# A decoder block: loading the first image by tiles, its low parts between the normalisations on VectorE, and unread products ahead

## The chip, the cores and the metric

The kernel runs on one core of a Trainium2 chip. The metric is the time of one execution on the device in microseconds, as the median of several runs; lower is better. Engine names: PE is TensorE, DVE is VectorE, ACT is ScalarE, POOL is GpSimd, SP is the engine that issues the transfers.

## What is computed

A decoder block on `x` of 4 images x 512 rows x 512 columns, in f32:

```python
x = x + attn(layernorm(x), Wq, bq, Wk, bk, Wv, bv, Wo, bo)   # 16 heads; attention over the 128 channels of a head
x = x + xattn(layernorm(x), ctx, ctx, gamma)                 # 8 heads
x = x + ffn(layernorm(x), w1, w3, w2)                        # ternary weights, silu(h1) * h3
```

In `attn` the queries are transposed, so that the scores of a head are q^T k over the 512 rows, a 128 x 128 matrix. With n = layernorm(x), these scores are Wq^T (n^T n) Wk and terms of the biases: the kernel first forms the Gram matrix n^T n (512 x 512) of each image and then multiplies it by the weights.

## The kernel before

Products keep f32 accuracy with rounded operands (type fp32r): each operand is split in a high part (ScalarE's copy, rounded) and a low part (operand minus high part), and `three_passes` makes high x high, high x low and low x high, so that lines 163, 164 and 165 stand for all such products. An attention pass takes two images (`PB` = 2); there are two passes, and cross attention and the feed-forward part follow.

The opening, which the change touches, is this, with an image as 4 row tiles j of 128 x 512 and a Gram matrix as 4 column blocks c:

- SP: `sp_rows_in` loads image 0 in two halves of two tiles each, then image 1 the same, then `raw_a` (wk), two rows for the bias, `raw_b` (wq), and more.
- GpSimd makes the identity `ident` (used for transposes later).
- VectorE, `dve_rows`: per tile statistics (`bn_stats`), their aggregate, the inverse root by 13 small dependent steps (`dve_rstd`, one for all four tiles), and then for each tile the normalisation and an addition of `KAPPA` to its first column (`dve_normalise`; this column carries the bias). ScalarE makes each tile's high part `ph` as soon as it is normalised (`act_rows`).
- The low parts `pl` of image 0 are made by VectorE after all four normalisations; those of image 1 by GpSimd (`pool_rows`), tile by tile as ScalarE's high parts come.
- TensorE: `pe_gram` for image 0, then image 1, with c outside and j inside: 4 x 4 x 3 = 48 products of 128 x 512 for an image. In the first block (c = 0) each tile j is waited for.
- The blocks leave PSUM as `gh` (ScalarE, `act_gram`) and `gl` (VectorE, `dve_gram`). ScalarE's order is: `ph` of image 0, `gh` of its blocks 0 and 1, `ph` of image 1, `gh` of blocks 2 and 3, the high part `wah` of wk, `gh` of image 1. VectorE's order: image 0's rows and low parts, image 1's rows, `gl` of image 0, the bias row added to wk (`dve_bias`), the low parts of two of the four blocks of wk (`dve_split_a`; GpSimd makes the other two), `gl` of image 1.
- Then TensorE goes to the products of wk with the Gram matrices (`pe_scores`). Four PSUM banks go round between all these tiles; a bank is free when VectorE has made the low part from it (`a_free`).

In the second pass the rows of both images are normalised between other work, and GpSimd makes all low parts; the change leaves that as it is.

Of the kernel before, what the change touches and what calls it, by code (L numbers as in the profile page):

```python
# [18 lines left out]
F32 = mybir.dt.float32  # L19
# [3 lines left out]
ALU = mybir.AluOpType  # L23
AX = mybir.AxisListType.X

P = 128
B, T, C = 4, 512, 512
CK = C // P
TJ = T // P
NH, HG = 16, 4  # L30
GROUPS = NH // HG
PB = 2
# [103 lines left out]
RSTD_STEPS = 1 + 12  # L136
# [31 lines left out]
def decoder_block(nc, x, ctx, wk, wq, wo, wvt, bk, bq, bv_col, bo, gamma, w1t, w3t, w2t, out):  # L168
# [7 lines left out]
    with stack:  # L176
# [2 lines left out]

        s = {}  # L180
        for name in (
            "ident", "xn_a0", "xn_b0", "xn_a1", "xn_b1", "raw_a", "raw_b", "row_in", "bv_in", "bo_in", "x_in", "wadd_a", "wadd_b",
            "link", "xn", "ph", "pl_dve", "pl_pool", "a_ready", "a_hi", "a_free",
            "wah", "wal_dve", "wal_pool", "wbh", "wbl",
            "s_done", "s_read", "mx", "nmx", "rinv", "dv", "vadd", "att_ready", "att_free", "pth", "ptl",
# [5 lines left out]
            "s_ready", "s_free", "t_ready", "t_free", "r_ready", "r_free",  # L191
            "xmx", "xrinv", "xpn", "pxh", "x3n", "x3h", "link_b",
            "tanh", "gate_sp", "gate_dve", "gate_pool", "y", "y_out",
        ):
            s[name] = sem("s_" + name)
# [121 lines left out]
        def late_bank(n):  # L317
            return bank[6 + n % 2]
# [656 lines left out]
        def sp_rows_in(sp, p, i):  # L975
            one, two = halves(x[PB * p + i])
            sp.dma_start(xnf[i][:, 0:2], one).then_inc(s[f"xn_a{i}"], 16)
            sp.dma_start(xnf[i][:, 2:4], two).then_inc(s[f"xn_b{i}"], 16)

        def sp_slot_a(sp, p, step):  # L980
            wait_raw_a_free(sp, p, step)
            src = wk[step] if step < GROUPS else wo[step - GROUPS]
            sp.dma_start(raw_a[:], src.rearrange("(c p) n -> p c n", p=P)).then_inc(s["raw_a"], 16)
# [161 lines left out]
        @block.sync  # L1145
        def _(sp):
            credit(sp, "sp")
            gate(sp, "sp")
            for i in range(PB):
                sp_rows_in(sp, 0, i)  # L1150
            sp_slot_a(sp, 0, 0)
            sp_row(sp, wk, bk, 0)
            sp_slot_b(sp, 0, 0)
            sp.dma_start(bvc[:], bv_col).then_inc(s["bv_in"], 16)
            for w in range(3):
                sp_magnitudes(sp, 0, w)
            sp.wait_ge(s["wadd_a"], wadd_a(0, 1))
            sp_row(sp, wq, bq, 0)
            sp.dma_start(gam[:], gamma.to_broadcast([P, 1])).then_inc(s["gam_in"], 16)
            sp_scores(sp, 0)  # L1160
            sp_values(sp, 0)
            sp_scores_early(sp)
            sp_values(sp, PASSES - 1)
            stage_b_sp(sp)
# [11 lines left out]
        def pe_gram(pe, p, i):  # L1176
            for c in range(CK):
                u = A["G", p, i, c]
                pe_bank(pe, u)
                for j in range(TJ):  # L1180
                    if c == 0:
                        if p == 0 and i == 0:
                            pe.wait_ge(s["pl_dve"], j + 1)
                        else:
                            pe.wait_ge(s["pl_pool"], TJ * (PB * p + i - 1) + j + 1)
                    mm = three_passes(pe, a_bank(u)[:], ph[:, i, j, c * P:(c + 1) * P], pl[:, i, j, c * P:(c + 1) * P],
                                      ph[:, i, j, :], pl[:, i, j, :], j == 0, j == TJ - 1)
                mm.then_inc(s["a_ready"], 1)
# [191 lines left out]
        def pe_values(pe, p):  # L1380
            for j in range(GROUPS):
# [9 lines left out]
                for i in range(PB):  # L1391
                    if last and further:
                        pe_gram(pe, p + 1, i)
                    for a in range(HG):
                        pe_out(pe, p, j, i, a)
                        if last and not further and i:
                            pe_x3(pe, 0, a)

        @block.tensor
        def _(pe):  # L1400
            pe.wait_ge(s["ident"], 2)
            for i in range(PB):
                pe_gram(pe, 0, i)
            pe_scores(pe, 0)
            pe_values(pe, 0)
            pe_scores_early(pe)
            pe_values(pe, PASSES - 1)
            stage_b_pe(pe)
# [243 lines left out]

        def dve_moments_in(dve, link, p, i, half):

            dve.wait_ge(s[("xn_a", "xn_b")[half] + str(i)], 16 * (p + 1))
            for j in (2 * half, 2 * half + 1):
                ins = dve.bn_stats(bst[:, i, j, :], xnf[i][:, j, :])
            link(ins)

        def dve_aggregate(dve, link, i):  # L1660
            for j in range(TJ):
                ins = dve.bn_aggr(mvar[:, i, j, :], bst[:, i, j, :])
            link(ins)

        def dve_rstd(dve, link, i, k):

            if k == 0:
                link(dve.tensor_copy(nvar[:, i], mvar[:, i, :, 1]))
            else:
                newton_step(dve, link, rstd[:, i], ntmp[:, i], nvar[:, i], k - 1)  # L1670

        def dve_normalise(dve, link, i, j):
            link(dve.tensor_scalar(xnf[i][:, j, :], xnf[i][:, j, :], mvar[:, i, j, 0:1], rstd[:, i, j:j + 1],
                                   ALU.subtract, ALU.mult))
            dve.tensor_scalar(xnf[i][:, j, 0:1], xnf[i][:, j, 0:1], KAPPA, None, ALU.add).then_inc(s["xn"], 1)

        def dve_rows(dve, link, p, i):
            for half in range(2):
                dve_moments_in(dve, link, p, i, half)
            dve_aggregate(dve, link, i)  # L1680
            for k in range(RSTD_STEPS):
                dve_rstd(dve, link, i, k)
            for j in range(TJ):
                dve_normalise(dve, link, i, j)

        def dve_low(dve, dst, high, u):
            dve.wait_ge(s["a_hi"], split(u))
            dve.tensor_tensor(dst, a_bank(u)[:], high.bitcast(F32), ALU.subtract).then_inc(s["a_free"], 1)  # L1688

        def dve_gram(dve, p, i):  # L1690
            for c in range(CK):
                dve_low(dve, gl[i][:, c, :], gh[i][:, c, :], A["G", p, i, c])

        def dve_row(dve, link, p, g, slot):
# [274 lines left out]
        @block.vector  # L1969
        def _(dve):  # L1970
            credit(dve, "dve")
            link = make_link(dve, "link", chain)
            dve_rows(dve, link, 0, 0)
            for j in range(TJ):
                dve.wait_ge(s["ph"], j + 1)
                dve.tensor_tensor(pl[:, 0, j, :], xnf[0][:, j, :], ph[:, 0, j, :].bitcast(F32), ALU.subtract).then_inc(s["pl_dve"], 1)
            dve_rows(dve, link, 0, 1)
            dve_gram(dve, 0, 0)
            dve_bias(dve, link, 0, 0, "a")
            dve_split_a(dve, 0, 0)  # L1980
            dve_gram(dve, 0, 1)
            dve_bias(dve, link, 0, 0, "b")
            dve_scores(dve, link, 0)
            dve_values(dve, link, 0)
            dve_scores_early(dve, link)
            dve_values(dve, link, PASSES - 1)
            stage_b_dve(dve, link)


        def pool_rows(pool, p, i):  # L1990
            for j in range(TJ):
                pool.wait_ge(s["ph"], TJ * (PB * p + i) + j + 1)
                pool.tensor_tensor(pl[:, i, j, :], xnf[i][:, j, :], ph[:, i, j, :].bitcast(F32), ALU.subtract).then_inc(s["pl_pool"], 1)
# [84 lines left out]
        @block.gpsimd  # L2078
        def _(pool):
            credit(pool, "pool")  # L2080
            pool.memset(ident[:], 0.0).then_inc(s["ident"], 1)
            pool.wait_ge(s["ident"], 1)
            pool.affine_select(out=ident[:], in_=ident[:], compare_op=ALU.not_equal, fill=1.0, base=0,
                               pattern=[[-1, P]], channel_multiplier=1).then_inc(s["ident"], 1)
            pool.memset(wsum[:], 0.0).then_inc(s["w_pad"], 1)
            pool_rows(pool, 0, 1)
            pool_split_a(pool, 0, 0)
            pool_split_b(pool, 0, 0)
            pool_scores(pool, 0)
            pool_values(pool, 0)  # L2090
            pool_scores_early(pool)
            pool_values(pool, PASSES - 1)
            stage_b_pool(pool)
# [34 lines left out]
```

## Time and profile before

| | us |
|---|---|
| median of 3 runs | 1137.38 (1136.97 to 1137.83) |
| the profiled execution, its time | 1134.82 |
| the same, its span | 1133.0 |
| TensorE busy in the span | 1108.6 |
| first product of TensorE | 14.01 |
| first product with wk | 37.26 |

The granted clock is 1.00 over the whole span. The span starts a little after the execution, hence the 1.8 us between its time and its span. Starts in the timeline are counted from the start of the span. The products overlap in the pipeline, so a product's pace is the distance of two starts, not its duration.

### The profile page before, as it was taken

The page shows a single profiled execution, that of the slowest core. Times are in us where ns is not written, and L with a number is a line of the kernel's source. Part 1 is how long each engine was busy: PE and PEld are TensorE (multiplying, and loading weights), DVE is VectorE, ACT ScalarE, POOL GpSimd, SP SyncE. Part 2 cuts the span into 40 slices and gives each one's busy share as a digit, 9 for nine tenths or more (in the row PEclk, how much of TensorE's full clock was granted, in tenths as well). Part 3 has the DMA queues.
Part 4 walks back from the last instruction along what each step waited for, and adds up shares of the span by engine and source line. Part 5 has one row for each costly group of instructions (what it writes and reads, how often), then busy time and mean ns, then how long its engine had stood idle before and what let it go on. Part 6 is the DMA issues. An engine that isn't in the chain of part 4 may idle for free.

```text
span 1133.0 us, 15861 instructions
## 1 busy us (share of the span) xinstructions
PE 1108.6 (98%) x5824; PEld 938.8 (83%) x5824; DVE 738.5 (65%) x1376; ACT 544.8 (48%) x1129; POOL 469.1 (41%) x412
## 2 busy tenths in 40 slices
PE   5999999999999999999999999999999999999998
PEld 4888888878888878888888888888888888888886
DVE  7555547787757578775524344689968876888532
ACT  3456673324242365676425142267727762776130
POOL 2222326341332265674352140156626752675131
PEclk9999999999999999999999999999999999999999
DMA  7455543544433722412630202462024111410000
GB/s 241 161 187 184 180 163 136 172 124 170 128 118 106 229 92 92 134 39 84 248 112 1 75 20 96 143 211 67 1 81 122 59 47 41 128 47 1 38 1 38
DMA packets 54376, 122.20 MB, mean 108 GB/s; under 512 B 10025, under 2 KB 10025, under 8 KB 52250
## 3 DMA queue, kind: packets, MB, share of 16 engines
q1 hardware_dynamic: 54298, 121.18, 32.7%
q8 instruction: 47, 0.77, 0.3%
q14 instruction: 31, 0.25, 0.1%
HBM read 103.32 MB, written 17.84 MB: 107 GB/s over the span
## 4 chain that ended last, share of the span: by engine, by line
PE 92%; DVE 4%; ACT 2%; issue 1%; DMA 0%; POOL 0%; DVEq 0%; POOLq 0%; SPq 0%
PE bank L163 19%; PE bank L165 19%; PE bank L164 19%; PE bank L575 6%; PE bank L576 6%; PE bank L535 4%; PE bank L590 4%; PE bank L591 4%; PE bank L557 3%; PE bank L558 2%; PE bank L545 2%; PE bank L546 2%; PE bank L600 1%; PE bank L523 0%; DVE xmx L760 0%
## 5 line engine op out<-in xcount | busy, mean ns | idle before, releaser
L575 PE MATMUL bank<-x3h,w 128*128 128x512 f32 (+2 forms) x368 | 143.3, 393 | 0.6 <-DVE x3l L847 0.3
L576 PE MATMUL bank<-x3l,w 128*128 128x512 f32 (+2 forms) x368 | 140.4, 384 | 0.0
L1420 ACT ACTIVATE yh<-bank 128x512 fp32r<-128x512 f32 x64 | 38.1, 600 | 209.9 <-PE bank L165 209.8
L929 POOL TENSOR_SCALAR pe_x<-pe_x,xri,gam 128x512 f32<-128x512 f32 x96 | 76.5, 797 | 99.1 <-DVE xri L764 95.9
L760 DVE TENSOR_REDUCE xmx<-bank 128x1 f32<-128x512 f32 x128 | 87.6, 686 | 30.8 <-PE bank L546 29.1
L1998 POOL TENSOR_TENSOR wal<-raw_a,wah 128x512 fp32r<-128x512 f32 x44 | 60.4, 1402 | 110.8 <-ACT wah L1442 110.8
L163 PE MATMUL bank<-wah,gh 128*128 128x512 f32 x256 | 102.8, 402 | 2.0 <-DVE wal L1728 2.0
L2003 POOL TENSOR_TENSOR wbl<-raw_b,wbh 128x512 fp32r<-128x512 f32 x64 | 87.6, 1396 | 39.0 <-ACT wbh L1462 38.7
L163 PE MATMUL bank<-yh,rh 128*128 128x512 f32 x256 | 100.2, 392 | 0.8 <-DVE xacc L1857 0.8
L163 PE MATMUL bank<-wah,ph 128*128 128x512 f32 x256 | 100.2, 391 | 0.0
L164 PE MATMUL bank<-wal,gh 128*128 128x512 f32 x256 | 100.1, 391 | 0.0
L165 PE MATMUL bank<-wah,gl 128*128 128x512 f32 x256 | 99.9, 390 | 0.0
L164 PE MATMUL bank<-wal,ph 128*128 128x512 f32 x256 | 99.8, 390 | 0.0
L165 PE MATMUL bank<-yh,rl 128*128 128x512 f32 x256 | 99.7, 389 | 0.0
L164 PE MATMUL bank<-yl,rh 128*128 128x512 f32 x256 | 99.7, 389 | 0.0
L165 PE MATMUL bank<-wah,pl 128*128 128x512 f32 x256 | 99.6, 389 | 0.0
L1688 DVE TENSOR_TENSOR yl<-bank,yh 128x512 fp32r<-128x512 f32 x64 | 44.1, 691 | 84.5 <-ACT yh L1420 84.5
L1857 DVE SCALAR_TENSOR_TENSOR xacc<-bank,rinv,xacc 128x512 f32<-128x512 f32 x64 | 47.9, 749 | 69.3 <-PE bank L165 66.9
L679 ACT ACTIVATE pe_x<-bank,xmx 128x512 f32<-128x512 f32 x96 | 66.1, 688 | 34.8 <-DVE xmx L760 34.5
L575 PEld LDWEIGHTS bank<-x3h,w 128*128 128x128 f32 (+1 forms) x368 | 68.2, 185 | 15.1 <-DVE x3l L847 0.7
L576 PEld LDWEIGHTS bank<-x3l,w 128*128 128x128 f32 (+1 forms) x368 | 68.2, 185 | 12.8
L1688 DVE TENSOR_TENSOR ml<-bank,mh 128x512 fp32r<-128x512 f32 x64 | 43.6, 686 | 53.8 <-ACT mh L1420 53.8
(172 smaller groups left out, 2997.8 us busy)
## 6 DMA issues: line engine op xcount, KB each, us to landing
raw_a<-in_wk SPq DMA_DIRECT2D x8, 1024.0 KB, 5.2
raw_b<-in_wq SPq DMA_DIRECT2D x8, 1024.0 KB, 5.6
raw_a<-in_wo SPq DMA_DIRECT2D x8, 1024.0 KB, 5.1
raw_b<-in_wvt SPq DMA_DIRECT2D x8, 1024.0 KB, 4.9
ternary_scratch<-wraw SPq DMA_DIRECT2D x24, 341.2 KB, 3.1
x1d<-x_scratch SPq DMA_DIRECT2D x48, 128.0 KB, 3.0
kd<-in_ctx SPq DMA_DIRECT2D x48, 128.0 KB, 3.2
w<-ternary_scratch SPq DMA_DIRECT2D x2, 2730.0 KB, 10.8
```

The source lines that it names most:

```text
L163: pe.matmul(out, wh, xh, start=start, stop=False, skip_group_check=shared)
L164: pe.matmul(out, wh, xl, start=False, stop=False, skip_group_check=shared)
L165: return pe.matmul(out, wl, xh, start=False, stop=stop, skip_group_check=shared)
L575: pe.matmul(u_bank[w][0:m, cols], lhs, x3h[:, c, cols], start=c == 0, stop=False)
L576: mm = pe.matmul(u_bank[w][0:m, cols], lhs, x3l[:, c, cols], start=False, stop=c == CK - 1)
L679: act.activation(m.pe_x[:, q, :], m.s[q % 2][:], ACT.Exp, bias=xmx[:, q:q + 1], accum_out=xrs[:, q:q + 1]).then_inc(s["s_free"], 1)
L760: dve.reduce_max(xmx[:, q:q + 1], m.s[q % 2][:], axis=AX, negate=True).then_inc(s["xmx"], 1)
L929: pool.tensor_scalar(m.pe_x[:, q, :], m.pe_x[:, q, :], xri[:, q:q + 1], gam[:], ALU.mult, ALU.mult).then_inc(s["xpn"], 1)
L1688: dve.tensor_tensor(dst, a_bank(u)[:], high.bitcast(F32), ALU.subtract).then_inc(s["a_free"], 1)
L1857: dve.scalar_tensor_tensor(xacc[:, i, a, :], late_bank(n)[:], rinv[:, j, a // 2, q:q + 1], xacc[:, i, a, :], ALU.mult, ALU.add).then_inc(s ...
L1998: pool.tensor_tensor(wal[:, c, :], raw_a[:, c, :], wah[:, c, :].bitcast(F32), ALU.subtract).then_inc(s["wal_pool"], 1)
L2003: pool.tensor_tensor(wbl[:, c, :], raw_b[:, c, :], wbh[:, c, :].bitcast(F32), ALU.subtract).then_inc(s["wbl"], 1)
```

## The change

- Image 0 comes in four transfers, one for each tile, each with its own semaphore; VectorE makes a tile's statistics as it lands. The order on SP is four tiles of image 0, two halves of image 1, and the rest as before.
- `dve_normalise_split`: normalise tile 0, tile 1, then low part 0, normalise 2, low part 1, normalise 3, low part 2, low part 3. It is used for image 0 and for image 1. GpSimd's `pool_rows(0, 1)` is gone; all eight low parts of the first pass are VectorE's.
- VectorE takes `gl` of blocks 0 and 1 of image 0 between the inverse root and the normalisations of image 1; blocks 2 and 3 come after them.
- TensorE, once `ident` is there, makes 22 products of `ident` with itself (unrounded f32, 128 x 128) into a bank that is first used later and whose content nobody reads, and then begins `pe_gram`.

```diff
+        def sp_first_rows(sp):
+
+            tiles = x[0].rearrange("(p j) c -> p j c", j=TJ)
+            for j in range(TJ):
+                sp.dma_start(xnf[0][:, j], tiles[:, j]).then_inc(s[f"xn_t{j}"], 16)
...
-            for i in range(PB):
-                sp_rows_in(sp, 0, i)
+            sp_first_rows(sp)
+            sp_rows_in(sp, 0, 1)
...
-                        if p == 0 and i == 0:
-                            pe.wait_ge(s["pl_dve"], j + 1)
+                        if p == 0:
+                            pe.wait_ge(s["pl_dve"], TJ * i + j + 1)
                         else:
-                            pe.wait_ge(s["pl_pool"], TJ * (PB * p + i - 1) + j + 1)
+                            pe.wait_ge(s["pl_pool"], TJ * i + j + 1)
...
+        def pe_warm(pe):
+
+            for k in range(22):
+                pe.matmul(late_bank(1)[:, 0:P], ident[:], ident[:], start=True, stop=True)
...
             pe.wait_ge(s["ident"], 2)
+            pe_warm(pe)
...
+        def dve_pl(dve, i, j):
+            dve.wait_ge(s["ph"], TJ * i + j + 1)
+            dve.tensor_tensor(pl[:, i, j, :], xnf[i][:, j, :], ph[:, i, j, :].bitcast(F32), ALU.subtract).then_inc(s["pl_dve"], 1)
+
+        def dve_normalise_split(dve, link, i):
+
             for j in range(TJ):
                 dve_normalise(dve, link, i, j)
+                if j:
+                    dve_pl(dve, i, j - 1)
+            dve_pl(dve, i, TJ - 1)
+
+        def dve_first_rows(dve, link):
+            for j in range(TJ):
+                dve.wait_ge(s[f"xn_t{j}"], 16)
+                ins = dve.bn_stats(bst[:, 0, j, :], xnf[0][:, j, :])
+            link(ins)
+            dve_aggregate(dve, link, 0)
+            for k in range(RSTD_STEPS):
+                dve_rstd(dve, link, 0, k)
+            dve_normalise_split(dve, link, 0)
+
+        def dve_second_rows(dve, link):
+            for half in range(2):
+                dve_moments_in(dve, link, 0, 1, half)
+            dve_aggregate(dve, link, 1)
+            for k in range(RSTD_STEPS):
+                dve_rstd(dve, link, 1, k)
+            dve_gram(dve, 0, 0, range(2))
+            dve_normalise_split(dve, link, 1)
...
-            dve_rows(dve, link, 0, 0)
-            for j in range(TJ):
-                dve.wait_ge(s["ph"], j + 1)
-                dve.tensor_tensor(pl[:, 0, j, :], xnf[0][:, j, :], ph[:, 0, j, :].bitcast(F32), ALU.subtract).then_inc(s["pl_dve"], 1)
-            dve_rows(dve, link, 0, 1)
-            dve_gram(dve, 0, 0)
+            dve_first_rows(dve, link)
+            dve_second_rows(dve, link)
+            dve_gram(dve, 0, 0, range(2, CK))
...
-            pool_rows(pool, 0, 1)
             pool_split_a(pool, 0, 0)
```

## Rows read from the trace of the kernel before

**Rows 1.** The page, part 1: busy us, share of the span, instructions.
```profile
PE 1108.6 (98%) x5824; PEld 938.8 (83%) x5824; DVE 738.5 (65%) x1376; ACT 544.8 (48%) x1129; POOL 469.1 (41%) x412
```

**Rows 2.** The waits of TensorE, whole span: us in total, times, longest.
```profile
PE bank L163 <- DVE pl L1976: 14.0, 1, 14.0
```

**Rows 3.** Timeline of TensorE in the opening: start, duration, instruction.
```profile
14.01 0.77 PE L163 MATMUL bank<-ph 128*128 128x512 f32 x1 [14.01 <-DVE pl L1976]
14.57 0.63 PE L164 MATMUL bank<-pl,ph 128*128 128x512 f32 x1
...
16.71 0.51 PE L163 MATMUL bank<-ph 128*128 128x512 f32 x1
...
18.19 0.39 PE L163 MATMUL bank<-ph 128*128 128x512 f32 x1
...
26.35 0.39 PE L163 MATMUL bank<-ph 128*128 128x512 f32 x1
...
37.26 0.39 PE L163 MATMUL bank<-wah,gh 128*128 128x512 f32 x1
```

**Rows 4.** SP's issues, times to landing of image 0's halves and of all, stretches' GB/s.
```profile
0.86 0.39 SPq L977 DMA_DIRECT2D xnf<-in_x  x1
...
2.24 0.43 SPq L978 DMA_DIRECT2D xnf<-in_x  x1
...
xnf<-in_x SPq DMA_DIRECT2D x1, 512.0 KB, 4.0
...
xnf<-in_x SPq DMA_DIRECT2D x1, 512.0 KB, 4.9
...
DMA to landing us min/median/max: 4.0/5.7/7.3
...
2.00:4.00 2.00, 0.00 (x0) 0.00 (x0) 0.00 (x0) 0.00 (x0) 0.00 (x0) 1.00 0.83 211
4.00:6.00 2.00, 0.00 (x0) 0.00 (x0) 1.07 (x2) 0.00 (x0) 0.00 (x0) 1.00 1.00 389
```

**Rows 5.** Timeline of VectorE and ScalarE, image 0.
```profile
4.93 2.63 DVE L1657 BATCH_NORM_STATS2 bst<-xnf 128x6 f32<-128x512 f32 x4 [4.93 <-DMA xnf<-in_x]
7.60 0.38 DVE L1662 BATCH_NORM_AGGREGATE mvar<-bst 128x2 f32<-128x6 f32 x4
...
10.60 0.55 DVE L1673 TENSOR_SCALAR xnf<-xnf,mvar,rstd 128x512 f32<-128x512 f32 x1
...
11.37 2.56 ACT L1416 ACTIVATE ph<-xnf 128x512 fp32r<-128x512 f32 x4 [9.37 <-DVE xnf L1675]
...
13.18 2.49 DVE L1976 TENSOR_TENSOR pl<-xnf,ph 128x512 fp32r<-128x512 f32 x4
```

**Rows 6.** Timeline of VectorE and GpSimd, image 1 and the blocks.
```profile
15.58 2.60 DVE L1657 BATCH_NORM_STATS2 bst<-xnf 128x6 f32<-128x512 f32 x4
...
21.22 0.55 DVE L1673 TENSOR_SCALAR xnf<-xnf,mvar,rstd 128x512 f32<-128x512 f32 x1
...
22.71 5.45 POOL L1993 TENSOR_TENSOR pl<-xnf,ph 128x512 fp32r<-128x512 f32 x4 [20.85 <-ACT ph L1416]
...
23.16 1.33 DVE L1673 TENSOR_SCALAR xnf<-xnf,mvar,rstd 128x512 f32<-128x512 f32 x1
...
24.60 1.96 DVE L1688 TENSOR_TENSOR gl<-bank,gh 128x512 fp32r<-128x512 f32 x3
...
33.99 2.08 DVE L1688 TENSOR_TENSOR gl<-bank,gh 128x512 fp32r<-128x512 f32 x3 [0.76 <-ACT gh L1420]
```

**Rows 7.** Timeline of GpSimd, the identity; and the chain of waits, transposes.
```profile
1.50 0.29 POOL L2083 TENSOR_SCALAR_AFFINE_SELECT ident<-ident 128x128 f32<-128x128 f32 x1 [0.50 <-POOL ident L2081]
...
91.50 0.87 PE bank L1236 x8
```

**Rows 8.** Timeline of TensorE after its longest later wait.
```profile
450.57 0.47 PE L163 MATMUL bank<-wah,gh 128*128 128x512 f32 x1 [1.97 <-DVE wal L1728]
450.87 0.39 PE L164 MATMUL bank<-wal,gh 128*128 128x512 f32 x1
```

More of the change, by code:

```diff
@@ L181, in decoder_block @@
         for name in (
-            "ident", "xn_a0", "xn_b0", "xn_a1", "xn_b1", "raw_a", "raw_b", "row_in", "bv_in", "bo_in", "x_in", "wadd_a", "wadd_b",
+            "ident", "xn_t0", "xn_t1", "xn_t2", "xn_t3",
+            "xn_a0", "xn_b0", "xn_a1", "xn_b1", "raw_a", "raw_b", "row_in", "bv_in", "bo_in", "x_in", "wadd_a", "wadd_b",
             "link", "xn", "ph", "pl_dve", "pl_pool", "a_ready", "a_hi", "a_free",
@@ L1653, in dve_moments_in @@
         def dve_moments_in(dve, link, p, i, half):
-            dve.wait_ge(s[("xn_a", "xn_b")[half] + str(i)], 16 * (p + 1))
+            dve.wait_ge(s[("xn_a", "xn_b")[half] + str(i)], 16 * (p + 1 if i else p))
             for j in (2 * half, 2 * half + 1):
@@ L1675, in dve_normalise @@
             dve.tensor_scalar(xnf[i][:, j, 0:1], xnf[i][:, j, 0:1], KAPPA, None, ALU.add).then_inc(s["xn"], 1)
[L1677 to L1682, printed above, removed]
+        def dve_pl(dve, i, j):
+            dve.wait_ge(s["ph"], TJ * i + j + 1)
+            dve.tensor_tensor(pl[:, i, j, :], xnf[i][:, j, :], ph[:, i, j, :].bitcast(F32), ALU.subtract).then_inc(s["pl_dve"], 1)
+        def dve_normalise_split(dve, link, i):
             for j in range(TJ):
                 dve_normalise(dve, link, i, j)
+                if j:
[18 more added lines that the diff above has]
+            dve_normalise_split(dve, link, 1)
         def dve_low(dve, dst, high, u):
@@ L1688, in dve_low, with dve_gram @@
             dve.tensor_tensor(dst, a_bank(u)[:], high.bitcast(F32), ALU.subtract).then_inc(s["a_free"], 1)
-        def dve_gram(dve, p, i):
-            for c in range(CK):
+        def dve_gram(dve, p, i, cs=range(CK)):
+            for c in cs:
                 dve_low(dve, gl[i][:, c, :], gh[i][:, c, :], A["G", p, i, c])
```

## The prediction

> **What bounds the kernel now.** I read the busy shares first: TensorE is busy for 1108.6 of 1133.0 us [rows 1]. Then the waits of TensorE: the largest by far is the first, 14.0 us until the first low part is there [rows 2]. The timeline of the opening shows that after it TensorE runs product on product: 96 gram products, then the first product with wk at 37.26 [rows 3]. So the time of the program is the time at which the products with wk begin, plus a long stretch set almost wholly by TensorE. I therefore predict one number, the shift of that 37.26, and carry it to the end. The few waits later (the longest is 1.97 us at 450.57 [rows 8]) hang on work that earlier products release, so they shift along.
>
> Inside the opening three speeds are to be seen [rows 3]. From 18.19 to 26.35 there are 36 products, 0.227 us each: full clock, 2.4 GHz. From 14.57 to 16.71 there are five intervals of 0.43 us: half clock, 1.2 GHz, after TensorE had done nothing since the start. The first 12 products (14.01 to 18.19) take 4.18 us where 12 x 0.227 = 2.72 would do: the slow start costs 1.46 us.
>
> **Load by tiles.** The two halves of image 0 land 4.0 and 4.9 us after their issues (the four issues for both images stand 0.46 us apart, from 0.86 to 2.24, so these two are at 0.86 and 1.32), at 4.86 and 6.2 [rows 4]; VectorE starts its statistics at 4.93 and needs four times 0.65 us [rows 5]. The same 1.05 MB now comes as four transfers. Tile 0: the first half (0.52 MB) lands when some 0.8 MB in all have been moved (0.42 MB by 4.0 us at 211 GB/s, then 389 GB/s [rows 4]), so a landing trails by 0.3 MB, and 0.26 MB would land near 4.3. The last tile: the bytes say 6.2 as now; its own issue at 2.24 plus the 4.9 us of the second half says 7.1. I take 6.2, since the transfers are limited by rate there, and keep 7.1. From 4.3, three statistics are done by 6.25, so the fourth starts at 6.25. From there the aggregate begins 7.60 - 4.93 - 3 x 0.65 = 0.72 us later, and the first normalisation 10.60 - 7.60 = 3.00 us after that [rows 5]: 9.97 instead of 10.60. The extra SP issues (0.46 us each) push everything behind them back by 0.9 us: the second image (its last half now lands at 2.24 + 7.3 = 9.5 [rows 4], needed at 15), wk and wq, which VectorE touches only after 27.8. Hidden, with many us to spare.
>
> **Low parts between the normalisations, image 0.** Count from the first normalisation, t. A normalisation with its one-column addition takes 0.65 (four of them fill 10.60 to 13.18), ScalarE's high part starts at t + 0.77 and takes 0.64, a subtraction takes 2.49 / 4 = 0.62, and the first product starts 14.01 - 13.18 = 0.83 after its subtraction begins [rows 3, 5]. Two normalisations end at 1.30, the first high part at 1.41, so the first subtraction starts at 1.45 where it started at 2.58. The rest is alternation: subtractions at 1.45, 2.72, 3.99 and, after the fourth high part (3.92 + 0.19 + 0.64), 4.79; VectorE is free at 5.41. TensorE gets its tiles at 2.28, 3.55, 4.82 and 5.62. So it starts at 12.25, not 14.01, but in steps of 1.27 us for three products, which need 0.68. The first column block ends at t + 5.62 + 0.68 = 16.27, against 18.19. Taken alone this is 1.9 us, and image 0 would end at 16.27 + 8.16 = 24.43 instead of 26.35.
>
> **Image 1: where the gain goes.** Before, its low parts are GpSimd's, 5.45 us from 22.71, done at 28.16 [rows 6]. TensorE needs the last of them at 26.35 + 9 x 0.227 = 28.39: just in time. Now VectorE makes them. Its chain: free at 9.97 + 5.41 = 15.38 (before 15.58: the alternation loses most of the head start); statistics, aggregate and the root take 21.22 - 15.58 = 5.64, to 21.02; two subtractions of gram blocks, put ahead, take 2 x 0.655 = 1.31 [rows 6], to 22.33; then the alternation again, its last tile at TensorE at 22.33 + 5.62 = 27.95. Three products (0.68) and 36 more (8.16) end at 36.79. TensorE, ready at 24.43, waits in between. One thing is given back and is already in this sum: a normalisation took 1.33 us instead of 0.54 while GpSimd was on its low parts [rows 6]; GpSimd is idle there now. Result: 37.26 - 36.79, a gain of 0.5 us.
>
> Behind it on VectorE: the last two gram blocks, the row and the additions to wk, the low parts of wk. They begin at 27.74 + 1.31 = 29.05, about 1.0 us later than the present after the faster row is counted, so image 1's first gram block is subtracted at 35.0 to 35.7 instead of 33.99 to 34.7 [rows 6]. It frees the bank for the first product with wk: 1.1 us before 36.79. That cover would be gone with another 1.1 us on VectorE alone. GpSimd's low parts of wk, released by the same chain, have their third block needed 1.4 us into that stretch, so they have more room.
>
> **The 22 products.** The identity is ready at 1.79 [rows 7]. The trace has no unrounded f32 product of 128 columns. From below: the transposes of the same size, 0.109 us each at full clock [rows 7], 0.22 at half. From above: four times that at half clock, 0.87. Between them lies a 512-column product at half clock, 0.43 [rows 3]. I take 0.43 until the clock rises (2.9 us of work, as from 14.01 [rows 3]) and half after: done near 8.3. That is before 12.25, so the price is nothing. The use is nothing either: if they leave the clock at full, the first block ends at 16.27; if not, three slow products take 1.29 us against steps of 1.27, and it ends some 0.3 us later; TensorE would still be at image 1 by 24.8, where it waits for VectorE until 27.95. The cover is that wait. The rule on the unrounded product, in the Trainium skill, "FP8 and Floating Point Precision", section "TensorE Precision Notes", is that true FP32 takes four passes through the array; by it my estimate would stand or grow to the upper bound, and by a one-pass transpose the products would be done sooner. No row here decides between them.
>
> **Sum.** On the profiled execution: 1134.82 - 0.5 = 1134.3. That execution is 2.6 us below the median of the three runs; I take the shift to hold for them too: 1137.38 - 0.5 = 1136.9 us. 0.2%, about what a measurement of this kernel can tell from no change, is 2.3 us.
>
> **Rivals.**
> VectorE sets the pace of image 1 (the forecast, 0.67). Its own range is the load's: last tile at 7.1 shifts all by 0.9 (a loss of 0.4); tiles so early that only 4 x 0.65 from 3.9 counts gives a gain of 0.9. So 1136.5 to 1137.8.
> TensorE is not held by image 1 (0.12): some of VectorE's chain is shorter than its rows say. Then 24.43 + 10.89 = 35.3, a gain of 1.9, 1135.4; with a load at its early bound 1135.0. Against it: every term of the chain has a row; for it, only that small gaps between instructions could close.
> The clock falls in the gaps (0.15). TensorE works 0.68 us of each 1.27 us in both first blocks. If it is back at half clock after image 1's, the slow start is paid again on the path, 1.46 us: a net loss of 1.0, 1138.4. For it: after idleness from the start the products are slow. Against: after 1.97 us idle the product at 450.87 shows 0.39 us, as those at full clock do, and not the 0.63 of half clock [rows 3, 8]. The Trainium skill, "TensorE: Matmul & The Clock Gate", section "HAM oscillation", says that bursts parted by waits for data are each begun at half rate; by it the sum is this rival's 1138.4, by the row it is 1136.9.
> The 22 products overrun (0.06), the rival on the other side. TensorE's queue is in order; if they end at s, the gram products cannot begin before. With s up to 15.0 nothing is lost (15.0 + 60 x 0.227 = 28.6, when VectorE lets the block end); from 37.26 - 96 x 0.227 = 15.5 on it is slower than before, which is 0.62 us for a product. At 0.87 for each of the 22, the clock never rising, s = 21.0 and the time is 1137.4 + 5.5 = 1142.9.
>
> **How the numbers follow.** Likeliest: 1136.9. Range for 8 in 10: from the second rival's 1135.3 to the clock's 1138.5. Faster by over 0.2%: half of the second rival and a little of the first, 0.08. Slower: most of the overrun and a clock that stays low for more than one slow start, 0.06. Same: 0.86.
>
> **What would show it.** The first tile's statistics near 4.3 and the first normalisation near 10.0; products of image 0 from about 12.3 in steps of 1.27 us; TensorE waiting for VectorE's low parts around 24.5 to 28; the first product with wk near 36.8. I am wrong if that product comes before 36 or after 38, if the first normalisation is later than 10.6, or if the identity's products still run at 13.

## The result

The changed kernel takes 1134.65 us (median of 20 runs, 1133.86 to 1136.60), the kernel before 1137.15 us (20 runs, 1135.36 to 1137.95). The ratio is 0.9981, with a 95% interval of 0.9975 to 0.9988: 2.5 us faster, about at the 0.2% (2.3 us) that the prediction names as what can be told from no change. The means of the same runs lie 2.07 us apart (1134.97 and 1137.04). The prediction was 1136.9 with a range of 1135.3 to 1138.5, so the measured time lies 0.65 us below the range. The profiled executions say the opposite of the medians: before 1134.82 (span 1133.0), after 1136.04 (span 1134.2). Which parts of the two differences belong to the kernels is what the runs below are for.

TensorE in the opening, after, as in [rows 3]:

```profile
1.85 7.31 PE L1409 MATMUL bank<-ident 128*128 128x128 f32 x44 [1.85 <-POOL ident L2115]
12.35 0.50 PE L163 MATMUL bank<-ph 128*128 128x512 f32 x1 [3.19 <-DVE pl L1692]
...
13.59 0.80 PE L163 MATMUL bank<-ph 128*128 128x512 f32 x1 [0.27 <-DVE pl L1692]
...
16.68 0.39 PE L164 MATMUL bank<-pl,ph 128*128 128x512 f32 x1
...
27.01 0.50 PE L163 MATMUL bank<-ph 128*128 128x512 f32 x1 [0.17 <-DVE pl L1692]
...
36.76 0.39 PE L163 MATMUL bank<-wah,gh 128*128 128x512 f32 x1
```

The first product with wk is at 36.76, where 36.79 was forecast, against 37.26 before. The 22 products are 44 instructions, two for each, and end at 9.16. Their starts are 0.213 us apart until about 6.2 and 0.112 after it, so that a product takes 0.43 us and then 0.22, as the prediction had taken it. The gram products begin at full clock at 12.35; then the clock falls near 13.2 and is back at 16.7, as the granted clock shows (0.58 from 13 to 14, 0.50 from 14 to 16). TensorE waits at image 1 only at 27.01, and for 0.17 us: with the fall in image 0 it comes there later than the 24.43 of the forecast, at 25.3. VectorE's side, as in [rows 5, 6], and the landing of tile 0 as in [rows 4]:

```profile
4.49 2.65 DVE L1705 BATCH_NORM_STATS2 bst<-xnf 128x6 f32<-128x512 f32 x4 [4.49 <-DMA xnf<-in_x]
7.17 0.38 DVE L1675 BATCH_NORM_AGGREGATE mvar<-bst 128x2 f32<-128x6 f32 x4
...
10.17 0.55 DVE L1686 TENSOR_SCALAR xnf<-xnf,mvar,rstd 128x512 f32<-128x512 f32 x1
...
15.49 2.60 DVE L1670 BATCH_NORM_STATS2 bst<-xnf 128x6 f32<-128x512 f32 x4
...
22.34 0.54 DVE L1686 TENSOR_SCALAR xnf<-xnf,mvar,rstd 128x512 f32<-128x512 f32 x1
...
26.27 1.47 DVE L1692 TENSOR_TENSOR pl<-xnf,ph 128x512 fp32r<-128x512 f32 x2
```
```profile
xnf<-in_x SPq DMA_DIRECT2D x1, 256.0 KB, 3.6
```

The chain of the forecast is there almost to the tenth (first normalisation 10.17 for 9.97, image 1's at 22.34 for 22.33). So the opening is 0.50 us shorter between these two executions, and yet this one's span is 1.2 us longer. The windows around the wait near 450 us, and TensorE's timeline behind it, show where that went; columns are the stretch, the five engines' busy time, granted clock, share and GB/s of the transfers:

```profile
440.00:449.00 9.00, 8.01 (x56) 7.17 (x54) 8.74 (x14) 6.24 (x14) 6.79 (x6) 1.00 0.22 59
449.00:456.00 7.00, 6.04 (x23) 5.02 (x24) 5.26 (x11) 2.35 (x10) 2.86 (x4) 0.76 0.60 217
```
```profile
449.96 0.66 PE L163 MATMUL bank<-wah,gh 128*128 128x512 f32 x1 [1.95 <-DVE wal L1763]
450.41 0.63 PE L164 MATMUL bank<-wal,gh 128*128 128x512 f32 x1
...
452.97 0.63 PE L164 MATMUL bank<-wal,gh 128*128 128x512 f32 x1
...
453.68 0.39 PE L163 MATMUL bank<-wah,gh 128*128 128x512 f32 x1
```

The same wait of 2 us stood in the kernel before [rows 8], with no loss of clock after it. Here the clock has fallen (the products are 0.43 us apart until 453.4), and 7.00 x 0.24 = 1.7 us are lost. From 36.76 on this execution takes 1097.4 us, the one of before took 1095.7. Two executions, then, differ by more than the change is worth, and the question became what an ordinary execution of each looks like.

### The profile page after: what moved, and what is told of

The parts are those of the page before. It is cut to its first block, busy times and chain, and to the rows that moved or that the text cites. A ratio compares the mean times of both kernels' runs of the same rounds, so it can differ in the third digit from the quotient of the medians.

```text
span 1134.2 us, 15950 instructions
## 1 busy us (share of the span) xinstructions
PE 1118.2 (99%) x5868; PEld 946.5 (83%) x5868; DVE 740.7 (65%) x1380; ACT 544.3 (48%) x1129; POOL 462.5 (41%) x408
## 4 chain that ended last, share of the span: by engine, by line
PE 88%; DVE 6%; ACT 2%; issue 2%; DMA 1%; SPq 0%; POOL 0%; DVEq 0%; POOLq 0%
PE bank L163 19%; PE bank L164 18%; PE bank L165 18%; PE bank L576 6%; PE bank L577 6%; PE bank L536 4%; PE bank L592 3%; PE bank L591 3%; PE bank L558 2%; PE bank L559 2%; PE bank L546 2%; PE bank L547 2%; DVE pxl L756 1%; PE bank L601 1%; DVE xmx L761 1%
```

## The experiments

"Against before" is the difference of the medians to runs of the kernel before on the same chip. E1 to E4 shared one chip, E5 to E8 a second, E9 to E12 a third; the median of before was 1136.92, 1137.30 and 1137.27 there. Each kernel has 7 to 11 runs. An interval is about 1 us wide to either side, so by these intervals alone a difference of less between two rows is not shown. "First wk" is the start of the first product with wk in that kernel's trace, which is one execution. The last column counts the runs whose mean granted clock is 1.000 or 0.999; a fall to half clock brings it to 0.998.

| run | median | against before | ratio, 95% interval | first wk | clock 1.000 or 0.999 |
|---|---|---|---|---|---|
| E1 before, again | 1137.14 | +0.2 | 1.0004 (0.9995 to 1.0013) | 39.15 | 1 of 11 |
| E2 before, 46 products ahead | 1136.26 | -0.7 | 0.9991 (0.9982 to 0.9999) | 37.76 | 4 of 11 |
| E3 changed, no products | 1134.46 | -2.5 | 0.9984 (0.9975 to 0.9992) | 37.33 | 8 of 11 |
| E4 changed, wait filled | 1134.40 | -2.5 | 0.9980 (0.9971 to 0.9989) | 36.81 | (falls in the opening) |
| E5 before, wait filled | 1136.63 | -0.7 | 0.9993 (0.9984 to 1.0002) | 38.03 | 11 of 11 |
| E6 before, 9 products in the path | 1138.25 | +1.0 | 1.0014 (1.0005 to 1.0023) | 39.74 | 6 of 11 |
| E7 changed, no products, wait filled | 1134.96 | -2.3 | 0.9980 (0.9970 to 0.9990) | 36.81 | 9 of 9 |
| E8 shared low parts | 1134.19 | -3.1 | 0.9971 (0.9961 to 0.9982) | 36.43 | 7 of 7 |
| E9 before, wait filled, load by tiles | 1135.63 | -1.6 | 0.9986 (0.9977 to 0.9995) | 36.95 | 10 of 11 |
| E10 before, wait filled, image 0 split | 1135.22 | -2.1 | 0.9982 (0.9973 to 0.9991) | 37.76 | 11 of 11 |
| E11 as E7, load in halves | 1135.23 | -2.0 | 0.9981 (0.9972 to 0.9990) | 37.55 | 11 of 11 |
| E12 before, wait filled, 46 products | 1134.98 | -2.3 | 0.9980 (0.9971 to 0.9989) | 37.59 | 11 of 11 |

**E1, the kernel before unchanged.**

> The kernel before, unchanged, to see its spread from run to run beside each run's granted clock. Theory A (clock): the profiled execution of before, 1134.8 us, was one in which the slow start was short (1.46 us) and the clock stayed up at the 2 us wait near 450 us. Other executions pay up to 1.7 us more at the start, where nothing hides it, and in part of them 1.7 us at 450, so the times lie between 1134.8 and 1138, with a median near 1137.1 and no single mode, and a new trace shows a later rise of the clock than 16.9 us or a fall at 450 us or both. Rival B (no clock; the profiled run was an outlier for another reason): a new trace shows the first product with wk at 37.3 again and the clock up at 450, and the extra time elsewhere.

TensorE's timeline of this execution, in the opening and around 453 us, VectorE's first normalisation, and the windows:

```profile
14.48 0.76 PE L163 MATMUL bank<-ph 128*128 128x512 f32 x1 [14.48 <-DVE pl L1976]
...
19.73 0.63 PE L163 MATMUL bank<-ph 128*128 128x512 f32 x1
...
20.53 0.40 PE L165 MATMUL bank<-ph,pl 128*128 128x512 f32 x1
...
39.15 0.39 PE L163 MATMUL bank<-wah,gh 128*128 128x512 f32 x1
...
452.47 0.47 PE L163 MATMUL bank<-wah,gh 128*128 128x512 f32 x1 [1.95 <-DVE wal L1728]
...
453.93 0.60 PE L163 MATMUL bank<-wah,gh 128*128 128x512 f32 x1
```
```profile
11.07 0.55 DVE L1673 TENSOR_SCALAR xnf<-xnf,mvar,rstd 128x512 f32<-128x512 f32 x1
```
```profile
449.00:456.00 7.00, 5.05 (x24) 4.18 (x24) 6.75 (x11) 3.18 (x12) 2.59 (x3) 0.85 0.42 143
456.00:465.00 9.00, 9.00 (x46) 7.48 (x45) 5.64 (x10) 5.82 (x18) 7.75 (x7) 0.92 0.48 177
```

Three things differ from the first profile. The halves land 0.5 us later (first normalisation 11.07, not 10.60 [rows 5]). The products stay at half clock from 14.48 to 20.2, twice as long as in [rows 3], so the first product with wk is at 39.15, 1.9 us later. And the clock falls near 453.9, here 1.4 us after the products have begun again; by the granted clock 7 x 0.15 + 9 x 0.08 = 1.8 us are lost. From the first product with wk on this execution takes 1097.2 us against 1095.7, so 1.4 of them reach the end. Of the 104 runs of the kernel before on the three chips (E1's included), 95 show a granted clock of 0.998, which is that of this execution. Their spans average 1135.5, those of the other nine 1134.1. Theory A holds: the first profile of before was an execution with a short slow start, an early load and no fall, all at once.

**E2, before with 46 unread products.** The kernel has this loop in a helper, `pe_warm`; here it is written out.

```diff
             pe.wait_ge(s["ident"], 2)
+            for k in range(46):
+                pe.matmul(late_bank(1)[:, 0:P], ident[:], ident[:], start=True, stop=True)
             for i in range(PB):
```

> Before, with 46 unread products of the identity ahead of the gram products and nothing else changed; at the pace seen for the 22 (7.31 us, the last passes 0.09 us apart) they end near 13.6 us, just before the first low part. Theory A: the whole slow start leaves the path: products begin at 14.0 at full clock, the first with wk at 35.8, and the median falls by 1.5 to 3.1 us, about 2.3, to 1134.9. Rival B (the slow start always costs what the profiled run showed): 1.5 us less, 1135.7. Rival C (the products heat nothing that lasts, or run past 14.0): no gain.

The slow start is gone: no gram product is at half clock. The products end at 14.04, and TensorE then still waits 0.48 us for VectorE, so they cost nothing. (The expectation's 0.09 us from one of their instructions to the next was a misreading; it is 0.11.) But the first product with wk is at 37.76, not at 35.8: with TensorE early, GpSimd's low parts of image 1 decide, as E12's rows show below. The price of a slow start is therefore only what reaches beyond them. 7 of 11 runs still have the fall. The gain in the median, 0.7, is below what either theory A or rival B forecast.

**E3, the changed kernel without its 22 products** (`pe_warm(pe)` left out).

> The changed kernel without the 22 products. Theory A: after the change TensorE waits for VectorE at image 1, so a slow start of any length is hidden there: the first product with wk stays at 36.8 and the median at 1134.65, within 0.3. Rival D (the gain is the products'): back by more than 1 us, to 1136 or above.

The median is 1134.46, the same as with them (1134.65 in other runs), so the products carry none of the gain, and rival D is out. The trace corrects the detail:

```profile
12.57 0.77 PE L163 MATMUL bank<-ph 128*128 128x512 f32 x1 [12.57 <-DVE pl L1691]
...
18.25 0.61 PE L164 MATMUL bank<-pl,ph 128*128 128x512 f32 x1
...
37.33 0.39 PE L163 MATMUL bank<-wah,gh 128*128 128x512 f32 x1
```

A slow start of 6 us reaches through VectorE's cover by 0.5 us (37.33 for 36.8). It is nearly hidden, not wholly.

**E4, the changed kernel with the wait near 450 filled.**

```diff
                 if c == 0 and i == 0:
+                    if p == PASSES - 1 and g == 2 and k == 0:
+                        for _ in range(10):
+                            pe.matmul(a_bank(u)[:, 0:P], ident[:], ident[:], start=True, stop=True)
                     wait_a(pe, p, g, k)
```

> The changed kernel with 10 unread products of the identity put into the 2.0 us wait near 450 us (ahead of the wait for the low parts of wk, third group of the second pass), into the bank that the next product clears. They need about 1.8 of the 2.1 us. Theory A: the clock cannot fall there any more; the runs that paid 1.7 us (9 of 20, those of 1135.5 and above) go over to the others, so the median falls by 0.5 to 0.8 us, to 1134.0, and no run is above 1135.2. Rival B (the two groups of times come from elsewhere): the spread of 2.7 us stays.

Ten of 11 runs lie between 1133.93 and 1134.72, one at 1137.28; without the filling 8 of 20 had spans of 1133.7 and more, and seven of these eight show a clock of 0.996 or 0.997, below the 0.998 that the fall in the opening alone brings (three of E4's 11 do so too). The median moves by only 0.25 where 0.5 to 0.8 was expected (the means, 1134.97 and 1134.59, by 0.4), since most runs of the changed kernel had no fall to lose. What the run at 1137.28 lost was not found.

**E5, the kernel before with the same edit.**

> The kernel before, with the 10 unread products in the 2 us wait near 450 us. So far 40 of 44 runs of before show a granted clock of 0.998, that is one fall, and both new traces of before's opening have it at 450 to 460; the changed kernel without products shows it in about 4 of 11. Theory A: the fall is what these runs share and it costs 1.7 us, so with the wait filled the clock is 1.000 in at least 10 of 11 runs and the median is 1.5 us below before's: 1135.4. What is left of the spread (1133 to 1136) is the length of the slow start. Rival B: the fall has another cause than the idle engine; clock 0.998 stays, no gain.

The clock is 1.000 in all 11 runs, so the idle engine is the cause of the fall. (Of the 71 runs with the wait filled and no fall in the opening, E5 and E7 to E12, one has it all the same: in E9, at 1139.26.) The gain is 0.7 us (0.8 in the means), half of what was expected. In its trace, products at half clock last from 14.49 to 18.0 and the first with wk is at 38.03. Its spans average 1134.6; with the 1096.2 us that follow the first product with wk in its own trace, that puts this product near 38.4 on average, where the first profile had 37.26. The nine runs of before that kept their clock without any filling average 1134.1, 0.5 less. Either the filling costs something or these nine had the shorter openings; which, no run shows.

**E6, the kernel before with 9 products in the path**, after the gram products (9 x `pe.matmul(late_bank(1)[:, 0:P], ident[:], ident[:])`).

> The kernel before, with 9 unread products between the gram products and those with wk: 1.65 us of TensorE work on the path, which moves the wait near 450 by that much after the rise of the clock in the opening, and nothing else. Theory E (locked): in before all TensorE work is paced by TensorE itself from the moment at which the clock rises to the wait at 450, so the wait always comes at the same distance from that rise, and that is why nearly every run has the fall; moved by 1.65 us, it goes from 0.9 of the runs to half of them or fewer, and the median is about before's, 1137.0 to 1137.5, in place of 1138.6. Rival (each run throws the dice at the wait, and before's dice are bad for a reason that lies near 450): the share of runs with clock 0.998 stays 0.9 and the median rises by the full 1.65, to 1138.6.

The share of runs at 0.998 goes from 95 of 104 (24 of 27 on this chip) to 5 of 11. So the wait's distance from the opening matters, as theory E says, and the rival's unchanged share is out. The median is between the two forecasts, +1.0: runs with the fall are at spans of 1137.8 to 1139.2, those without at 1135.5 to 1136.5, farther apart than one fall. The trace, of a run with the fall, shows something that the expectation had ruled out ("and nothing else"). First this trace, VectorE and TensorE, then VectorE in the first profile of before:

```profile
340.18 0.69 DVE L1700 SCALAR_TENSOR_TENSOR rowb<-rowb 128x512 f32<-128x512 f32 x1 [7.06 <-DMA rowb<-in_wk]
...
349.35 0.50 PE L163 MATMUL bank<-yh,rh 128*128 128x512 f32 x1 [1.27 <-DVE xacc L1859]
```
```profile
336.37 0.69 DVE L1698 SCALAR_TENSOR_TENSOR rowb<-rowb 128x512 f32<-128x512 f32 x1 [5.75 <-DMA rowb<-in_wk]
```

The row of wk for the second pass comes later here, VectorE's chain behind it is late, and TensorE stands 1.27 us for it, where no such wait is longer than 0.5 us in the other traces. Whether the other four runs with the fall have this wait too is not shown.

**E7, the changed kernel without its products, wait filled.**

> The changed kernel without its 22 products at the start and with the 10 in the wait near 450: no fall can be there, and no products of the identity disturb the record of the clock in the opening. Theory A: clock 1.000 in nearly all runs, spans 1132.2 to 1132.8, median 1134.3. Against before with the wait filled (1135.4) this leaves what the opening itself is worth, 1.1 us: 0.5 by the order of the work, as in the two profiled runs, and 0.6 as the mean of slow starts longer than the profiled one, which VectorE now hides. Rival F (the slow start was never longer than profiled, and before's extra time is the fall alone): 0.5 us apart.

1.7 us below E5 on the same chip (the means give 1.6). Between the two only the opening differs, both are free of the fall, and no run of E7 (at most 1135.40) is as long as the shortest of E5 (1135.42). Rival F's 0.5 is refuted: in ordinary executions the new opening is worth three times what the two profiles show. Not all of it has been gained by the first product with wk: by the mean spans and what follows that product in the two traces (1096.2 and 1095.7), it comes 1.1 us earlier on average, and 0.5 us come behind it. A part of these is small waits such as this one of E5, which E7 and the first profile do not show:

```profile
346.50 0.50 PE L163 MATMUL bank<-yh,rh 128*128 128x512 f32 x1 [0.20 <-DVE xacc L1860]
```

**E8, low parts of image 1 shared.** The cut shows VectorE's and GpSimd's side. TensorE's waits follow it; besides, 36 unread products stand ahead in place of 22, and the wait near 450 is filled.

```diff
-            dve_gram(dve, 0, 0, range(2))
-            dve_normalise_split(dve, link, 1)
+            dve_gram(dve, 0, 0, range(1))
+            for j in range(TJ):
+                dve_normalise(dve, link, 1, j)
+            dve_pl(dve, 1, 2)
+            dve_pl(dve, 1, 3)
...
+            for j in range(2):
+                pool.wait_ge(s["ph"], TJ + j + 1)
+                pool.tensor_tensor(pl[:, 1, j, :], xnf[1][:, j, :], ph[:, 1, j, :].bitcast(F32), ALU.subtract).then_inc(s["pl_pool"], 1)
```

> The changed kernel with three more things: 36 products at the start in place of 22 (they end near 11.7), the low parts of image 1 shared (GpSimd makes tiles 0 and 1, VectorE 2 and 3, after its four normalisations), and the wait near 450 filled. Theory A: TensorE starts at 12.4 at full clock and is not held by image 1 any more: first product with wk at 35.6 in place of 36.8, median 1.2 below the previous kernel of this call: 1133.1. Rival G (VectorE is then late with the bank of image 1's first gram block, or with wk): the first product with wk at 36.2 or later.

The lowest median of all: 0.8 below E7 on the same chip, 3.1 below before. The first product with wk is at 36.43, later than the 35.6 of theory A, so rival G's threshold is met, but not by its bank. The rows of TensorE, VectorE and GpSimd show it:

```profile
24.76 0.47 PE L163 MATMUL bank<-ph 128*128 128x512 f32 x1
...
26.09 0.50 PE L163 MATMUL bank<-ph 128*128 128x512 f32 x1 [0.40 <-POOL pl L2130]
```
```profile
23.11 2.93 POOL L2130 TENSOR_TENSOR pl<-xnf,ph 128x512 fp32r<-128x512 f32 x2 [21.25 <-ACT ph L1436]
...
23.56 1.33 DVE L1693 TENSOR_SCALAR xnf<-xnf,mvar,rstd 128x512 f32<-128x512 f32 x1
...
25.00 2.19 DVE L1699 TENSOR_TENSOR pl<-xnf,ph 128x512 fp32r<-128x512 f32 x2
```

While GpSimd subtracts (23.11 to 26.04), VectorE's normalisation takes 1.33 us for 0.54 and two subtractions 2.19 for 1.3. TensorE stands twice, ahead of 24.76 and of 26.09, for GpSimd's two low parts, 1.47 us each. VectorE's two, slow as they are, come in time: the products of their tiles begin at 26.90 and 27.59 without a wait.

**E9 and E10, one part each on the kernel before.** E9 takes `sp_first_rows` and the statistics tile by tile; E10 takes the alternation of normalisations and low parts for image 0 alone.

> The kernel before with the wait near 450 filled (as e5, which stood 0.7 us below before) and image 0 loaded by tiles, nothing else. In four further traces of before the first normalisation is at 11.0 to 11.2, not at 10.60 as in the first profiled run, since the halves land 0.5 us later; with tiles it is at 10.1 to 10.3 in five traces. Theory H (the load is the larger part): first normalisation 10.2, everything of the opening 0.9 us earlier, median 0.9 below e5's, 1.6 below before: 1135.5. Rival (the load is worth the 0.43 us of the two first profiles): 0.4 below e5, 1136.0.

```profile
10.36 0.55 DVE L1682 TENSOR_SCALAR xnf<-xnf,mvar,rstd 128x512 f32<-128x512 f32 x1
```
```profile
13.77 0.77 PE L163 MATMUL bank<-ph 128*128 128x512 f32 x1 [13.77 <-DVE pl L1991]
...
36.95 0.39 PE L163 MATMUL bank<-wah,gh 128*128 128x512 f32 x1
```

1.0 below E5 by the medians (0.7 to 0.8 by the means), nearer to theory H's 0.9 than to the rival's 0.4; the medians alone, on two chips, would not part the two. The traces do: the first normalisation is at 10.36 for E5's 11.08, 0.7 us earlier. The first product with wk is 1.1 us earlier, of which 0.3 is a shorter slow start (3.0 us for 3.5).

> As e5, and image 0's low parts between its normalisations, loads in halves, image 1's low parts still GpSimd's. TensorE starts 1.1 us earlier (13.4) and works off the slow start in the steps of 1.27 us, but VectorE gets to image 1 0.4 us later, and GpSimd's last low part sets the first product with wk at 38.2 whatever the length of the slow start. Theory A: in e5 this was the later of 37.75 (GpSimd) and TensorE's own 36.3 plus half the slow start's length (37.7 to 39.1), so the median changes by -0.4 to +0.2 against e5: 1136.2 to 1136.6, and the spread shrinks. Rival (the split by itself is worth the 1.1 us by which TensorE starts earlier): 1135.4.

TensorE's first product, its first with the last tile of image 1 and its first with wk; GpSimd's low parts of image 1:

```profile
13.12 0.76 PE L163 MATMUL bank<-ph 128*128 128x512 f32 x1 [13.12 <-DVE pl L1978]
...
28.79 0.50 PE L163 MATMUL bank<-ph 128*128 128x512 f32 x1
...
37.76 0.39 PE L163 MATMUL bank<-wah,gh 128*128 128x512 f32 x1
```
```profile
23.30 5.43 POOL L2006 TENSOR_TENSOR pl<-xnf,ph 128x512 fp32r<-128x512 f32 x4 [21.43 <-ACT ph L1419]
```

The median is 1.4 below E5's (the means 1.1 to 1.2) where theory A expected -0.4 to +0.2; the rival's 1135.4 is the number that fits. Its mechanism is not: TensorE starts 1.4 us earlier than in E5, but GpSimd's last low part, done at 28.73, holds it, and the first product with wk gains 0.3 on E5's trace (37.76, where 38.2 was forecast). The spread shrinks as forecast (1134.98 to 1135.79). What was wrong is the size: E5's first product with wk is near 38.4 on average, so that 0.7 us are gained up to it, and some 0.3 us behind it, where E5's trace takes 1096.2 us and this one 1095.9.

**E11 and E12.** E11 is E7 with the load in halves, E12 is E2 and E5 together.

> As e7 (the changed kernel without the products at the start, with the wait near 450 filled) but image 0 loaded in halves again. Theory H: first normalisation back at 11.1, first product with wk at 37.7 in place of 36.8, median 0.9 above e7's, 1.4 below before: 1135.7. Rival: 0.4 above e7.

0.3 above E7 by the medians, 0.74 by the first product with wk (37.55 for 36.81). Theory H's 0.9 does not come out of the medians, the rival's 0.4 does; in these two traces H's 37.7 for the first product with wk does (37.55). With tiles TensorE starts earlier into its slow start, which can then reach through the cover, as in E3; that this makes the load worth less here than in E9 is argued, not shown.

> As e5, and 46 unread products ahead of the gram products: no slow start, no fall at 450. Theory A: the first product with wk stands at 37.75, set by GpSimd's low parts, in every run; in e5 it lay at 37.75 to 39.1; so the median falls by 0.6 against e5, to 1135.8, and the spread is that of the load alone, below 1.2 us. Rival (the slow start is short, as in the first profile): no change against e5.

TensorE's waits and GpSimd's low parts of image 1:

```profile
25.73 0.50 PE L163 MATMUL bank<-ph 128*128 128x512 f32 x1 [0.23 <-DVE gl L1697]
28.58 0.50 PE L163 MATMUL bank<-ph 128*128 128x512 f32 x1 [0.28 <-POOL pl L2002]
...
37.59 0.39 PE L163 MATMUL bank<-wah,gh 128*128 128x512 f32 x1
```
```profile
23.10 5.42 POOL L2002 TENSOR_TENSOR pl<-xnf,ph 128x512 fp32r<-128x512 f32 x4 [21.25 <-ACT ph L1425]
```

1.6 below E5 by the medians, 1.3 to 1.4 by the means, where 0.6 was forecast; ten of the 11 runs lie within 0.6 us, one 1.1 us above them. The first product with wk is where theory A had it (37.59 for 37.75). By the mean spans and the rest of each trace, 0.6 to 0.8 us are gained up to that product, which is the price of the slow start beyond GpSimd's pace in the kernel before. The other 0.7 lie behind it (1095.5 us for E5's 1096.2) and are not explained beyond the small waits of E5. Products of the identity alone win all this back, with nothing of the change but them, if they last until the first low part.

## Why the prediction was wrong

**What bounds the kernel** was right in the main: after the first product with wk, E3, E4, E7, E8, E11 and E12 take 1095.3 to 1095.7 us, as the first profile's 1095.7. E10, E5 and E9, free of a fall too, take 1095.9, 1096.2 and 1096.4. So the rest of the kernel is not constant either: it moves by up to 1.1 us, as much as some of the terms below.

**The chain of the change** was right: 36.76 for 36.79, with VectorE's terms to 0.2 us, and the 22 products with neither use nor price worth naming (E3). Their pace was the one assumed, 0.43 us and then half. Their end was at 9.16 for 8.3 (the prediction's own terms give 8.0), since the half clock lasted until about 6.2 and not 4.7, far from the 15.0 from which they cost. The Trainium skill, "FP8 and Floating Point Precision", section "TensorE Precision Notes", has four passes for true FP32; the trace shows two instructions for each of the 22, 0.112 us apart at full clock, where a transpose of the same size takes 0.109. So a product took two transposes' time and not the four of the upper bound; how many passes an instruction stands for, no run here shows.

**The step that failed** is in the sum: "I take the shift to hold for them too". The shift was that of one execution, and three of its terms were at their lucky ends. The 2.6 us between that execution and the median should have been a warning. The shift in the medians was 2.5 us for the forecast 0.5.

- "The slow start costs 1.46 us": it lasts from 2.9 us (first profile) to 5.8 (E1) in the traces of before. In the first profile TensorE's path and GpSimd's came out level at 37.26, so that none of a longer slow start was covered. Its price beyond GpSimd's pace is 0.6 to 0.8 us on average at the first product with wk, and up to 1.6 with what comes behind it (E5 to E12). VectorE's pace in the changed kernel hides nearly all of it (E3), and the split alone hides it behind GpSimd's pace (E10).
- "The two halves land at 4.86 and 6.2": in the seven further traces with halves (E1, E2, E5, E6, E10 to E12) VectorE's statistics start 0.3 to 0.6 us later, while with tiles they start within 0.1 us of the changed kernel's profile. The load is worth 0.7 to 1.0 us on the kernel before (E9) and 0.3 to 0.7 on the changed one (E11).
- "The few waits later shift along": in time they do, but the clock behind the one near 450 does not. 95 of 104 runs of before show the clock of a fall, and about 4 in 10 of the changed kernel have one by spans of 1133.7 and above. At 1.4 us (E1) to 1.7 us (the changed kernel's profile) for a fall that would be 0.7 to 0.9 us.

**The sum that the runs give**: the opening 1.6 (E5 to E7; 1.1 of it at the first product with wk), of which the load and the hidden slow start are not separable by adding, since the later of two paths decides; fewer falls 0.7 to 0.9; together 2.3 to 2.5, where the medians show 2.5 and the means 2.07. The second term is the weaker one: filling the wait brought before 0.7 to 0.8 us, where 0.91 x 1.4 to 1.7 = 1.3 to 1.5 was due, and the changed kernel 0.25 to 0.4, where 0.6 to 0.7 was due. Taken from the filling, in means, the falls are worth 0.79 - 0.38 = 0.4 us between the two kernels, and with 1.56 for the opening the sum is 2.0, near the 2.07. What a fall costs in one execution and what its removal brings are thus 0.6 us apart in the kernel before, and that gap is open. Why the fall comes in nearly every run of before is shown as far as the distance from the opening matters (E6, with the reservation of its trace, and E2, where without a slow start it came in 7 of 11).

**The rivals.** "The clock falls in the gaps" came true in another place: in the opening it fell in image 0's first block, where it cost nothing, and near 450 it falls in both kernels. I had set the 1.97 us of [rows 8] against the rule of the Trainium skill, "TensorE: Matmul & The Clock Gate", section "HAM oscillation"; one wait that passed without a fall was an execution's chance: 95 of 104 runs of before show the clock of a fall. The waits for data in that section are longer than this one. Of half rate from the start of the burst, as the prediction tells the rule, the traces show both: the changed kernel's burst at 449.96 begins at half pace, E1's begins at full pace at 452.47 and falls 1.4 us later. The second rival (TensorE not held by image 1) and the overrun did not happen. The range's lower end was given as the second rival's 1135.3, where that rival's own figures are 1135.4 and 1135.0; neither reaches the 1134.65.

## What to carry to other kernels

Before a shift read from one trace is carried to the median, look at how far that execution lies from the median: a gap as large as the effect says that the trace is not the ordinary case, and the terms that can vary (landing of the first loads, length of the slow start, clock after each wait of some 2 us) need their range, most of all where two paths come out level in it. Where another engine paces the first ten microseconds of TensorE's work, a slow start of TensorE is nearly hidden (E3, E10). Unread products did the same when they lasted until the real ones began (46 in E2 and E12), and not when they ended 3 us before (22 in the changed kernel). And a wait of 2 us in a stretch that TensorE sets was followed by a loss of another 1.4 to 1.7 us of clock in most runs of before, which ten unread products in it prevented in 70 of 71 runs.

## What the runs showed of the hardware

- The clock can fall after the work has resumed: in E1 near 453.9, 1.4 us after the end of a 2 us wait; in the changed kernel near 13.2, 0.9 us after products had begun again at full clock.
- The granted clock reads 1.00 over an opening whose products go at half pace (0.43 us apart), so the slow start is to be read from the products' distances.
- A 128-column unrounded f32 product is two instructions, 44 for 22, with starts 0.213 us apart at half clock and 0.112 at full (4 to 5 and then 8 to 9 starts in a microsecond, before and after 6.2 us in the changed kernel's trace).
- Beside GpSimd's subtraction VectorE's own, of two tiles in SBUF, takes 1.1 us for 0.65, and its normalisation 1.33 for 0.54 (E8). VectorE's subtraction from a PSUM bank is not slowed: 1.96 us for three while GpSimd subtracts [rows 6], 0.65 each.
- The time from the first products to full clock is not fixed: in traces whose first products are the gram products it is 2.9 to 6.1 us (shortest in the first profile, longest in E3).
